# Two-layer graph attention on one core: the scaled row chunks of heads 1 to 7 move from GpSimd to VectorE, one chunk at a time

## What is computed

```
Wh = einsum('nf,hfd->hnd', x, W_heads)
s1 = einsum('hnd,hd->hn', Wh, a1); s2 = einsum('hnd,hd->hn', Wh, a2)
e = s1[:, :, None] + s2[:, None, :]
e = where(e > 0, e, 0.2 * e); e = where(adj > 0, e, -9e15)
hp = elu(einsum('hnm,hmd->hnd', softmax(e), Wh))
x = layernorm(x + hp_of_all_heads @ W_out + b_out)
```

## Time and profile before

| | us |
|---|---|
| median of 3 runs | 2718.33 |
| lowest and highest run | 2714.97, 2719.56 |
| profiled execution, its own time | 2718.68 |
| its span | 2716.8 |
| mean granted TensorE clock | 0.996 of full speed |

### The profile page before, as it was taken

How to read it: one execution, slowest core, us unless ns; L and a number is a source line. 1 busy time by engine, 2 the same in 40 slices (tenths; PEclk the granted TensorE clock), 3 DMA queues, 4 the chain that set the end, 5 groups by cost and what they waited for, 6 DMA issues and landing times.

```text
span 2716.8 us, 62711 instructions
## 1 busy us (share of the span) xinstructions
PE 2636.0 (97%) x26553; PEld 2338.9 (86%) x26553; DVE 1969.4 (72%) x3206; ACT 2070.2 (76%) x3253; POOL 573.3 (21%) x479
## 2 busy tenths in 40 slices
PE   8889999999999999999999999999999989999998
PEld 6558887888888888888888888888888889999998
DVE  6546678776776776767777677675555679989898
ACT  5457876777877778787777877778763569999997
POOL 1220026232331422323232242230002320000000
PEclk9999999999999999999999999999999999999999
DMA  9985421110110111111011011102114555333330
GB/s 348 371 304 173 158 89 45 31 30 20 44 28 27 38 31 30 34 31 30 24 41 27 27 38 35 27 19 56 38 34 167 195 185 206 109 117 114 105 133 18
DMA packets 196384, 243.07 MB, mean 89 GB/s; under 512 B 14853, under 2 KB 125448, under 8 KB 196106
## 3 DMA queue, kind: packets, MB, share of 16 engines
q1 hardware_dynamic: 196106, 239.07, 27.1%
HBM read 180.45 MB, written 57.74 MB: 88 GB/s over the span
## 4 chain that ended last, share of the span: by engine, by line
PE 73%; DVE 12%; ACT 9%; DMA 3%; issue 2%; SPq 1%; POOL 0%; ACTq 0%; DVEq 0%; POOLq 0%
PE l_ps L785 54%; PE l_ps L894 9%; ACT l_arena L1023 5%; PE l_ps L822 4%; DMA l_wh<-l_arena 2%; PE l_ps L752 2%; DVE l_arena L1378 2%; DVE l_arena L1377 2%; ACT l_arena L1112 2%; DVE l_arena L1573 1%; PE l_ps L847 1%; DVE l_arena L1572 1%; PE l_ps L810 1%; DVE l_arena L1561 1%; DVE l_arena L1399 1%
## 5 line engine op out<-in xcount | busy, mean ns | idle before, releaser
L785 PE MATMUL l_ps<-l_arena 128*128 128x258 f16 x16384 | 1808.3, 273 | 9.9 <-DVE l_arena L1378 5.9
L785 PEld LDWEIGHTS l_ps<-l_arena 128*128 128x128 fp8e4 x16384 | 1602.3, 98 | 213.5 <-DVE l_arena L1378 10.3
L1023 ACT ACTIVATE l_arena<-l_arena 128x512 fp8e4<-128x512 f32 x2048 | 1281.7, 708 | 73.7 <-PE l_ps L785 71.6
L1377 DVE SCALAR_TENSOR_TENSOR l_arena<-l_arena,l_mask 128x512 uint32<-128x512 uint32 x512 | 459.4, 897 | 397.2 <-ACT l_arena L1023 393.9
L1378 DVE TENSOR_TENSOR l_arena<-l_arena,l_mask 128x512 uint32<-128x512 uint32 x512 | 488.1, 953 | 0.0
L894 PE MATMUL l_ps<-l_arena 128*128 128x130 f16 x8000 | 462.3, 221 | 24.3 <-DVE l_arena L1581 11.7
L894 PEld LDWEIGHTS l_ps<-l_arena 128*128 128x128 fp8e4 x8000 | 456.4, 98 | 30.1 <-DVE l_arena L1573 25.3
L1112 ACT ACTIVATE l_arena<-l_arena 128x1024 fp8e4<-128x1024 f32 x434 | 457.4, 1141 | 3.3 <-PE l_ps L894 3.2
L409 POOL TENSOR_TENSOR l_arena<-l_arena 128x516 f32<-128x516 f32 x119 | 156.3, 1314 | 1188.6 <-PE l_ps L785 1131.2
L1041 ACT COPY l_arena<-l_ps 128x258 f32<-128x258 f32 x256 | 93.4, 369 | 241.0 <-PE l_ps L785 241.0
L1383 DVE SCALAR_TENSOR_TENSOR l_arena<-l_ps,l_arena 128x258 f32<-128x258 f32 x256 | 117.0, 481 | 141.4 <-ACT l_arena L1041 141.4
(11 more groups left out here) (164 smaller groups left out, 1288.2 us busy)
## 6 DMA issues: line engine op xcount, KB each, us to landing
l_arena<-in_adj SPq DMA_DIRECT2D x128, 512.0 KB, 6.5
l_arena<-uv SPq DMA_DIRECT2D x125, 272.0 KB, 5.5
l_arena<-l_wh SPq DMA_DIRECT2D x64, 256.0 KB, 4.6
l_arena<-l_srow SPq DMA_DIRECT2D x64, 256.0 KB, 3.2
feat<-l_arena SPq DMA_DIRECT2D x64, 256.0 KB, 2.3
l_arena<-feat SPq DMA_DIRECT2D x32, 512.0 KB, 3.9
l_wh<-l_arena SPq DMA_DIRECT2D x64, 192.0 KB, 8.2
uv<-l_arena SPq DMA_DIRECT2D x8, 1088.0 KB, 5.2
```

The source lines that it names most:

```text
L785: last = nc.tensor.matmul(sums(t, m), pattern(k, m).bitcast(F8)[:, j, t * P:(t + 1) * P], uv[:, slot(h, order[k]) + j, m * WH:m * WH + 2 * ...
L1023: ins = act.activation(pattern(k, 0).bitcast(F8)[:, j, :], s1b[q][:, :], ACT.Relu, bias=kc[:, h, jt:jt + 1], scale=STEEP, saturate=False)
L1377: dve.scalar_tensor_tensor(c, v, ONE8X4, m, ALU.bitwise_xor, ALU.bitwise_and)
```

## The change

The table `releases` and GpSimd's part in heads 1 to 7 go. A table `spots` gives each chunk of heads 1 to 7 a sweep and a turn, and VectorE makes the chunk there, behind that turn's split. An entry (b, m) stands for sweep 8 (h - 1) + b, so b = 8 is the first sweep of the chunk's own head. A chunk is now two products rounded to f16, then eight fused multiply-subtracts of 129 columns, with no f32 product in between. Head 0 and `fetch`, the table of SP's loads, stay as they are.

```diff
-    releases = [[0] * CPB, [50, 52, 54, 57, 59, 61, 66, 67]] + [[12, 20, 28, 36, 44, 59, 61, 66]] * (H - 2)
+    spots = [(), ((6, 1), (6, 3), (6, 5), (7, 0), (7, 2), (7, 4), (8, 1), (8, 3))] + [
+        ((1, 2), (2, 2), (3, 2), (4, 2), (5, 2), (7, 4), (8, 1), (8, 3))] * (H - 2)
+    scaled_at = {((h - 1) * NB + b, m): (h, c) for h in range(1, H) for c, (b, m) in enumerate(spots[h])}
...
-            for h in range(H):
-                make(h)
+            def make(c):
+
+                k = c % 4
+                pool.wait_ge(s_wh[k], 16 * (c // 4 + 1))
...
+                nc.gpsimd.tensor_tensor(tv[:, :, :], whx[k][:, :, :], factor(ev, 0, c), ALU.mult)
+                nc.gpsimd.tensor_tensor(part(0, c, 2), whx[k][:, :, :], factor(ev, 0, c), ALU.mult).then_inc(s_pl, 1)
...
+            for c in range(CPB):
+                make(c)
...
-            def make_high(c):
...
+            def make_next(h, c):
+
+                k, n = c % 4, 2 * CPB + (h - 1) * CPB + c
+                dve.wait_ge(s_wh[k], 16 * (2 * h + c // 4 + 1))
+                if c >= TWIN:
+                    dve.wait_ge(s_pe, HC * (h - 1) + HC - CPB + (3 if c == TWIN else 2))
+                elif h > 1:
+                    dve.wait_ge(s_pe, HC * (h - 1))
+                else:
+                    dve.wait_ge(s_mt, UNITS)
+                dve.tensor_tensor(part(h, c, 0), whx[k][:, :, :], factor(eu, h, c), ALU.mult)
+                dve.tensor_tensor(part(h, c, 2), whx[k][:, :, :], factor(ev, h, c), ALU.mult).then_inc(s_ud, 1)
                 dve.wait_ge(s_ud, n + 1)
...
+                for f, p in ((eu, 0), (ev, 2)):
+                    for j in range(JC):
+                        ins = dve.scalar_tensor_tensor(part(h, c, p + 1)[:, j, :], whx[k][:, j, :],
+                                                       f[:, h, c * JC + j:c * JC + j + 1], part(h, c, p)[:, j, :],
+                                                       ALU.mult, ALU.subtract)
+                ins.then_inc(s_uv, 1)
...
-                    if g == NB and m == 3:
-                        make_high(CPB - 1)
+                    if (g, m) in scaled_at:
+                        make_next(*scaled_at[g, m])
                     if m == 0 and g > 0:
                         add_exponentials(g - 1)
```

More of the change, by code:

```diff
@@ L388, in _ @@
                 nc.gpsimd.memset(whx[k][:, :, :], 1.0).then_inc(s_one, 1)
[L390 to L419, removed]
@@ L420, in _ @@
-            for h in range(H):
-                make(h)
+            def make(c):
+                k = c % 4
+                pool.wait_ge(s_wh[k], 16 * (c // 4 + 1))
+                if c > 0:
+                    pool.wait_ge(s_uv, c)
+                else:
+                    pool.wait_ge(s_f, 2)
+                    pool.wait_ge(s_ro, 16)
+                if c == 4:
+                    pool.wait_ge(s_pd, WIDE)
+                nc.gpsimd.tensor_tensor(tv[:, :, :], whx[k][:, :, :], factor(ev, 0, c), ALU.mult)
+                nc.gpsimd.tensor_tensor(part(0, c, 2), whx[k][:, :, :], factor(ev, 0, c), ALU.mult).then_inc(s_pl, 1)
+                pool.wait_ge(s_pl, c + 1)
+                pool.wait_ge(s_ud, 2 * c + 2)
+                nc.gpsimd.tensor_tensor(part(0, c, 3), tv[:, :, :], part(0, c, 2), ALU.subtract).then_inc(s_uv, 1)
@@ L1351, in make @@
                 dve.tensor_tensor(part(0, c, 1), tu[:, :, :], part(0, c, 0), ALU.subtract).then_inc(s_ud, 1)
-            def make_high(c):
[L1355 to L1358, removed]
-                dve.wait_ge(s_ud, n + 1)
[L1360 to L1364, removed]
+            def make_next(h, c):
[5 more added lines that the diff above has]
+                    dve.wait_ge(s_pe, HC * (h - 1))
+                else:
+                    dve.wait_ge(s_mt, UNITS)
+                dve.tensor_tensor(part(h, c, 0), whx[k][:, :, :], factor(eu, h, c), ALU.mult)
+                dve.tensor_tensor(part(h, c, 2), whx[k][:, :, :], factor(ev, h, c), ALU.mult).then_inc(s_ud, 1)
+                dve.wait_ge(s_ud, n + 1)
+                for f, p in ((eu, 0), (ev, 2)):
[4 more added lines that the diff above has]
+                ins.then_inc(s_uv, 1)
             def split(g, k):
```

## The result

| | before | changed |
|---|---|---|
| median of 5 runs, us | 2719.56 | 2709.51 |
| lowest and highest | 2714.97, 2722.38 | 2706.58, 2714.71 |
| profiled execution, its own time | 2718.68 | 2714.71 |
| its span | 2716.8 | 2712.9 |

The ratio is 0.997, with a 95% interval of 0.9958 to 0.9982: a gain of 5 to 11 us, 8 in the middle, against a forecast of 8.4 (2710.3 us). The two medians are 10.0 us apart. These times can't tell 8.4 from 9 or 10. The profiled execution of the changed kernel is the slowest of its five. So spans are a poor measure here, and I read one stretch instead: from TensorE's start of sweep 6 to its first transpose behind sweep 63. It holds 14848 matmuls, 1633.3 us at the pace of 0.11.

The account below looks back on a forecast made before the run. TensorE, busy 97%, bounds the kernel, so only its stops or slowing count. Gone 7.47 + 1.67 + 6 x 0.15 = 10.04 us, added 1.67, net -8.4 on 2718.68: 2710.3 us, range 2707 to 2717.

Parts of the forecast that it names:

- The 7.47 us of stops and 1.67 us of clock: Sweeps 6 to 8: TensorE's five stops, 7.47 us, and slow clock behind the last, 1.67 us, both forecast to go.
- The 6 x 0.15 us of the later heads: Starts of heads 2 to 7: TensorE lacks 0.15 us at each of six, forecast to go.
- The price of 3.45 us a chunk: VectorE: two products, then eight fused instructions at 0.265 us each (2.12 us), 3.45 us in all per chunk.
- The losses of 0.49 and 1.18 us in sweep 7: Sweep 7, turns 0, 2, 4: positions 3 and 7 ready late, 0.49 and 1.18 us lost, 1.67 us added once.
- All places that I called hidden: Chunks in sweep 6, b = 7, b = 8 and turn 2 cost TensorE nothing, with 0.0 to 1.5 us left.
- +21.1, +24.4 and +26.9: Sweep 6, us from TensorE's start: position 7 ready, third chunk ended, next two splits ended, ahead of +28.16.
- The two rules on the price: Skill's pipe-emptying rule advises few instructions; its column figures give 0.209 us a piece; the prediction took the trace's 0.265.
- Thin margins: Rival 1: at 3.75 us a chunk, places with 0.0 to 0.4 us left overflow: 2714.3 us; 0.24 together with rival 4.
- The clock falling in sweep 7: Rival 2: the 1.18 us stop in sweep 7 lowers the clock, +1.67 us, 2712.0 us, still faster; chance 0.08.
- Fused instructions that do not overlap: Rival 3: each fused instruction holds VectorE 0.346 us, a chunk costs 4.15 us, 2724.2 us, slower; chance 0.08.
- Stops in spite of a silent GpSimd: Rival 4: order, not contention, makes the stops, so they stay: 2719.4 us; 0.24 together with rival 1.
- VectorE's busy time level: Sign in the new profile: 56 chunks put in 233 us and the shorter splits take out about as much.

Follow-up runs that it names:

- the run with head 1 alone: Changed kernel with only head 1's chunks on VectorE, GpSimd keeping heads 2 to 7 with the old releases: 2708.39 us, ratio 0.9964.
- the runs with each half: Two runs: VectorE makes only head 1's chunks (2708.39 us), or only those of heads 2 to 7 (2715.04 us); GpSimd makes the others as before.
- The run with 0.8 us more per chunk: Changed kernel plus three more fused instructions per chunk into scratch that nobody reads: 2728.09 us, ratio 1.0034.
- 0.3 us more a chunk: Changed kernel with chunks made on VectorE by six instructions over 516 columns in place of the fused form: 2714.07 us, ratio 0.9986.
- the odd turns: Changed kernel with chunks 3, 4 and 5 of head 1 at turns 1, 3, 5 of sweep 7 instead of 0, 2, 4: 2708.23 us, ratio 0.9962.
- GpSimd made busy: Changed kernel with GpSimd doing six f32 products of 512 columns into scratch at each old chunk place: 2882.86 us against 2717.58 for before.
- later heads alone: Changed kernel with only heads 2 to 7 on VectorE, head 1 on GpSimd with the shared chunk 7 as before: 2715.04 us, ratio 0.999.

## Why the prediction was right

**The bound.** Right. Only TensorE's stops counted. VectorE's share went from 72 to 70% and GpSimd's from 21 to 4%, and the time moved by 0.3%.

**What goes.** The 7.47 us of stops and 1.67 us of clock at head 1's start are gone; the run with head 1 alone shows them. The 6 x 0.15 us of the later heads was mis-sized, by half. The stretch before lost 1644.3 - 1633.3 = 11.0 us, of which 1.9 lay there, and the runs with each half show 1.9 from both sides. The windows show the 0.15 us in which TensorE was idle. But the prediction's own rule for rows is that a row ends 0.165 us later than the next matmul could start, so an idle gap of 0.15 is a delay of 0.32, and 6 x 0.32 = 1.9. One of the six stops, on TensorE's timeline of the kernel before:

```profile
1566.93 458.09 PE L785 MATMUL l_ps<-l_arena 128*128 128x258 f16 x4160 [0.15 <-DVE l_arena L1378]
```

Hence 9.4 us in place of the 8.4 forecast. That is an error of a tenth, which the times of the runs can't show.

**What comes.** The price of 3.45 us a chunk is met to the hundredth. The losses of 0.49 and 1.18 us in sweep 7 came as 0.53 and 1.15. All places that I called hidden were, among them those with a tenth of a microsecond left. For sweep 6 the prediction has 0.1 to 0.2 us too much by its own steps (+21.1, +24.4 and +26.9 add up to +21.0, +24.3 and +26.7): its third chunk ran from +20.8 to +24.3.

**The two rules on the price.** The rows decided and were right: eight fused instructions of 0.347 us each lie in 2.19 us. By the Trainium skill's sentence on the pipe it would have been 2.8. The prediction quotes half of what that section of the Trainium skill (VectorE: DVE Perf Modes, The DRAIN you can't avoid) says: it goes on that a next instruction that is not held starts earlier, and the trace agrees with that half (0.265 us from start to start at a length of 0.347). The run with 0.8 us more per chunk shows what it would have been without this overlap: slower than before.

**The rivals.** Thin margins: they are thin, since 0.3 us more a chunk took 5.8 us back, and 0.8 us took 19; but the price left them whole. In both runs the layout came out a little low, by 0.1 to 0.2 us a head. The clock falling in sweep 7: not behind 1.15 us. Fused instructions that do not overlap: excluded. Stops in spite of a silent GpSimd: only the two forecast in sweep 7 were left, the odd turns removed those too, and GpSimd made busy brought stops back with the same order.

**A miss beside the time.** I had VectorE's busy time level. It fell by 60 us. I had added up the lengths of the fused instructions (0.346 x 448 = 155 us) where the profile's busy time counts their overlaps once: 123.0. By the lines the splits gave back 241 us (947.5 to 706.6) and the chunks put in 201. The other 20 us I have not followed; lines count the overlap of neighbouring instructions twice and the engine's sum does not.

## What to carry to other kernels

Work moved onto an engine with time to spare costs nothing only where its place in that engine's order leaves the next due instruction its time: lay one sweep out from starts and needs, and price the moved piece from instructions of its own shape. A stop that is moved may come back behind the next thing that the engines wait for, as in sweep 0, so compare from one fixed event to another and not the row alone. A helper engine can slow another engine's instructions while both run (0.69 to 1.52 us here), so one at 21% can be the cause of the bottleneck's stops. For a gain of a few tenths of a per cent, compare a stretch between two fixed events of the traces, whose repeat here was within 0.1 us, and let several executions average the rest.

## What the runs showed of the chip beyond that

- Whether the clock falls behind a stop is partly chance. The 2.0 us stop of sweep 0 was followed by a fall (1.7 us, a clock of 0.57 over 4 us) in three of nine profiled executions that have it; the changed kernel had it in one of its two. Stops of 2.72 to 2.76 us were followed by one in three of three (before, later heads alone, three more instructions), a stop of 2.4 us with GpSimd busy was not (in one execution), and stops up to 1.79 us in none.
- GpSimd can be held up by VectorE too: one of its instructions took 4.45 us where others of its kind take 1.1 to 1.5, while VectorE issued six split instructions back to back at 0.68 us each (460.61 to 464.30), without being slowed. In other places both were slowed. Which of the two gives way was not tried by itself.
